# Perceiver block on one core: another order of the last product's parts on TensorE

## The chip, the cores and the metric

The kernel runs on one core of one Trainium2 chip. The metric is the device time of one execution in microseconds (us), as a median over runs. The core has five engines with queues of their own: TensorE (PE in the profile, its weight loads PEld), VectorE (DVE), ScalarE (ACT), GpSimd (POOL) and SyncE (SP, which issues the DMAs here). They meet by semaphores alone.

## The reference

Three residual steps over `x` of 2 batches x 128 rows x 2048 columns, all in float32: a product with a context after both were quantised, one layer of attention, and a product with 4-bit weights.

```python
x = x + xattn(layernorm(x), ctx)     # fake_quant(layernorm(x)) @ fake_quant(ctx)
x = x + attn(layernorm(x), Wq, Wkv, Wo)
# the last one, which the change is in:
zq = unpack4(qzeros, 2048) + 1
W = scales[g_idx] * (wq - zq[g_idx])           # 16 groups of 128 rows
x = x + (einsum('bsi,io->bso', layernorm(x), W) + bias)
```

## The kernel before, in words

TensorE multiplies in a rounded float32 format (FP32R). For accuracy each float32 operand is split in an upper part (the rounded value) and a lower part (the remainder), and a product is three matmuls: upper x upper, upper activations x lower weights, lower activations x upper weights. They add up in one PSUM bank (128 rows x 512 float32 columns; there are 8).

The last product has K = 2048 in 16 steps j of 128. Step j needs a **granule** of weights, 128 x 2048 upper (`hi_slots`) and 128 x 2048 lower (`lo_slots`), in a ring of five slots (four in `w_hi` and `w_lo`, the fifth in `xt_hi` and `xt_lo`). VectorE makes both: `ffn_upper(j)` (L865) multiplies the nibbles by the rounded scales, `ffn_lower(j)` (L870) by what the rounding left; they count `f_hi_set` and `f_lo_set`. ScalarE takes 8 off the nibbles before (L556). `hd_hi` and `hd_lo` hold the normalised rows, transposed: per batch 16 transposes on TensorE (`transposes`, L993) into four banks, ScalarE rounds each bank (L430), VectorE takes the remainder (L616).

One **granule of work**, `f_granule(j, b)`, is 12 matmuls of 128 x 512 for batch b: three parts of four matmuls, one for each 512-column chunk n, in bank 4b + n. The parts come in the order upper x upper, upper activations x lower weights, lower activations x upper weights. The last four matmuls of step 15 count `ffn_done`, one for each chunk. VectorE waits for each count, adds the bank to `resid` (L942), and SyncE stores the chunk (L336), 256 KB.

The zero points come in as a correction of low rank: `row_sums` (L1120, 32 matmuls of 128 x 256) sums the transposed rows by group into bank 7. Its first matmul waits until VectorE has written all of `hd_lo` for both batches. ScalarE reads the sums (L575), VectorE reads and combines them (L930, L931, which counts `rs_out`), and `correction` (L1144) multiplies them by a small table. Bank 7 also belongs to batch 1's last chunk, so `f_granule(0, 1)` waits for `rs_out`.

The order on each engine is written out by hand, as the order of the calls. On TensorE it is here: step 0 and step 1 of batch 0, the transposes of batch 1, the row sums, step 2 of batch 0, then (after `rs_out`) step 0 of batch 1, the correction, steps 1 and 2 of batch 1, steps 3 to 11 for both batches in turn, steps 12 to 15 of batch 0, steps 12 to 15 of batch 1. On VectorE `ffn_upper(2)` stands ahead of the four remainders of batch 1, `ffn_lower(2)` behind them.

Of the kernel before, what the change touches and what calls it, by code (L numbers as in the profile page):

```python
# [15 lines left out]
P = 128  # L16
B = 2
D = 2048
KT = D // P
CH = 512  # L20
NCH = D // CH
# [22 lines left out]
W_Q, W_O, W_F, W_END = 0, 16, 32, 48  # L44
# [4 lines left out]
def slot_of(w):  # L49

    return w % RING if w < W_O else (w - W_O) % (RING + 1)
# [14 lines left out]
def perceiver(nc, x, ctx_in, s1, z1, s2, z2, wq, wkv, wo, qweight, qzeros, scales, bias, out):  # L66
# [6 lines left out]
    with ExitStack() as ec:  # L73
        def sb(name, shape, dt):
            return ec.enter_context(nc.sbuf_tensor(name, shape, dt))

        def sem(name):
            return ec.enter_context(nc.semaphore(name))
# [22 lines left out]
        hd_hi = sb("hd_hi", [P, KT, B * P], F32R)  # L101
        with nc.sbuf_tensor("at", [P, KT, B * P], BF16) as at, nc.sbuf_tensor("q16", [P, 2, D], BF16) as q16:
            pass
        hd_lo = sb("hd_lo", [P, KT, B * P], F32R)
# [59 lines left out]
        hi_slots = [w_hi[:, s] for s in range(RING)] + [xt_hi[:].rearrange("p k m -> p (k m)")[:, 0:D]]  # L164
        lo_slots = [w_lo[:, s] for s in range(RING)] + [xt_lo[:].rearrange("p k m -> p (k m)")[:, 0:D]]
        raw_slots = [raw[:, s] for s in range(RING)] + [raw_fifth[:]]

        bank = ec.enter_context(nc.psum_tensor("bank", [P, 8, CH], F32))
# [44 lines left out]
        f_lo_set = sem("f_lo_set")  # L213
# [34 lines left out]
        ffn_done = sem("ffn_done")  # L248
# [11 lines left out]
        def tr_bank(n, g):  # L260
            if n == 0:
                return g % 3
            return 1 + g % 3 if n == 1 else 4 * (n % B) + g
# [682 lines left out]
        def _(pe):  # L946
            mm = nc.tensor.matmul
# [30 lines left out]
            def transposes(n):  # L978
                b = n % B
                pe.wait_ge(norm_set, n + 1)  # L980
                for t in range(KT):
                    g = t // 4
                    if n < B:
                        rows = work[:, b, :].rearrange("m (p t) -> m t p", t=KT)[:, t, :]
                    else:
                        h, r = divmod(t, PACK)
                        j = r // 2 + 4 * (r % 2)
                        rows = work[:, b, :].rearrange("m (h p j) -> m h j p", h=HALVES, j=PACK)[:, h, j, :]
                    if n < B and t == 12:
                        pe.wait_ge(lo_out, 4 * n + 1)  # L990
                    if n == 1 and t == 0:
                        pe.wait_ge(colsum_out, B)
                    ins = nc.tensor.transpose(bank[:, tr_bank(n, g), (t % 4) * P:(t % 4 + 1) * P], rows, ident[:])  # L993
                    if t % 4 == 3:
                        ins.then_inc(tr_done, 1)
# [119 lines left out]
            def row_sums():  # L1115
                pe.wait_ge(masks_set, 3)
                pe.wait_ge(lo_out, 4 * B + UNITS + 8)
                for k in range(KT):
                    for part in (hd_hi, hd_lo):
                        ins = mm(bank[:, 7, 0:B * P], group_of[:, k // PACK, :], part[:, k, :],  # L1120
                                 start=k == 0 and part is hd_hi, stop=k == KT - 1 and part is hd_lo)
                ins.then_inc(rs_done, 1)

            def f_granule(j, b):
                w, m = W_F + j, slice(b * P, (b + 1) * P)
                hi, lo = hi_slots[slot_of(w)], lo_slots[slot_of(w)]
                pe.wait_ge(f_hi_set, j + 1)
                pe.wait_ge(lo_out, 4 * B + UNITS + 4 * (b + 1))
                for left, right, first, last in ((hd_hi, hi, True, False), (hd_hi, lo, False, False),
                                                 (hd_lo, hi, False, True)):  # L1130
                    if right is lo:
                        pe.wait_ge(f_lo_set, j + 1)
                    for n in range(NCH):
                        ins = mm(bank[:, 4 * b + n, :], left[:, j, m], right[:, n * CH:(n + 1) * CH],  # L1134
                                 start=first and j == 0, stop=last and j == KT - 1)
                        if last and j == KT - 1:
                            ins.then_inc(ffn_done, 1)
                if b == B - 1 and j < KT - 1:
                    ins.then_inc(w_used, 1)

            def correction():
                for b in range(B):
                    for n in range(NCH):
                        mm(bank[:, 4 * b + n, :], rsum[:, b * P:(b + 1) * P], corr_r[:, n * CH:(n + 1) * CH],  # L1144
                           start=False, stop=False)
# [34 lines left out]
            for n in range(1, NCH):  # L1180
                ua, ub = 2 * n - 2, 2 * n - 1
                w = W_Q + 4 * n
# [49 lines left out]
            o_granule(15, 1)  # L1232

            f_granule(0, 0)
            f_granule(1, 0)
            transposes(3)
            row_sums()
            f_granule(2, 0)
            pe.wait_ge(rs_out, 1)
            f_granule(0, 1)  # L1240
            pe.wait_ge(corr_split, 1)
# [4 lines left out]
                f_granule(j, 0)  # L1246
                f_granule(j, 1)
            for b in range(B):
                for j in range(KT - 4, KT):
                    f_granule(j, b)  # L1250


_INS = ['x', 'ctx_4096', 'L0_xattn_x1_scale', 'L0_xattn_x1_zp', 'L0_xattn_x2_scale', 'L0_xattn_x2_zp',
# [19 lines left out]
```

## Time and profile before

| | before |
|---|---|
| median of 3 runs | 447.43 us |
| lowest, highest | 444.41, 447.49 us |
| profiled execution, its own time | 447.83 us |
| its span (first to last instruction) | 446.1 us |
| PE busy | 381.2 us (85%) |
| DVE busy | 322.4 us (72%) |
| ACT busy | 219.5 us (49%) |
| mean granted TensorE clock | 0.972 |

The span is shorter than the time by 1.7 us, which lie outside the first and last instruction. Busy shares are averages over stages with different limits. The last product fills the stretch from 344 us to the end.

### The profile page before, as it was taken

How to read it: one execution, taken by the hardware profiler on the slowest of the kernel's cores; microseconds unless marked ns; L12 is line 12 of the kernel's file. 1: busy time of each engine (PE TensorE's matmuls, PEld its weight loads, DVE VectorE, ACT ScalarE, POOL GpSimd, SP SyncE). 2: the span in 40 equal slices, each digit the busy share in tenths (PEclk: the TensorE clock that was granted, in tenths of full speed). 3: DMA queues.
4: the chain of work that ended last, by engine and by line, in shares of the span. 5: the costliest groups of instructions: out<-in, count | busy, mean ns of one | idle time of the engine just before them, and what ended most of it. 6: DMA issues, size and time to landing. Idle time of an engine off the chain costs nothing.

```text
span 446.1 us, 4684 instructions
## 1 busy us (share of the span) xinstructions
PE 381.2 (85%) x1836; PEld 280.8 (63%) x1836; DVE 322.4 (72%) x316; ACT 219.5 (49%) x266; POOL 38.2 (9%) x75
## 2 busy tenths in 40 slices
PE   0285667666999999999999999977989899999995
PEld 0121222213778886877877868855768788888884
DVE  4698896759702794794764948549999999999822
ACT  2887986993204595375573824123904233444000
POOL 8994000000000000000000001000000000000000
PEclk9999999969799999999999999988999999999999
DMA  6999999991035443443436416999400000000022
GB/s 284 423 422 421 405 412 424 422 389 70 1 97 205 181 153 131 131 154 122 162 133 244 135 54 157 195 250 389 180 1 1 1 0 0 1 0 1 0 94 94
DMA packets 24273, 77.43 MB, mean 174 GB/s; under 512 B 1626, under 2 KB 1802, under 8 KB 19210
## 3 DMA queue, kind: packets, MB, share of 16 engines
q1 hardware_dynamic: 24092, 77.01, 47.9%
q8 instruction: 14, 0.23, 0.2%
q10 hardware_dynamic: 160, 0.13, 0.1%
q14 instruction: 7, 0.06, 0.0%
HBM read 74.91 MB, written 2.10 MB: 173 GB/s over the span
## 4 chain that ended last, share of the span: by engine, by line
PE 57%; DMA 17%; DVE 9%; ACT 8%; SPq 5%; issue 4%; POOLq 0%; DVEq 0%; POOL 0%
PE bank L1134 19%; DMA raw<-in_ctx 11%; PE bank L1000 9%; PE bank L1002 9%; PE bank L1001 9%; DMA raw<-in_L_attn_Wo 5%; ACT q L417 4%; DVE w_lo L625 2%; PE bank L1062 2%; PE bank L1087 2%; SPq L325 2%; SPq L321 2%; PE bank L1075 1%; PE bank L1030 1%; DVE stats L595 1%
## 5 line engine op out<-in xcount | busy, mean ns | idle before, releaser
L625 DVE TENSOR_TENSOR w_lo<-raw,w_hi 128x2048 fp32r<-128x2048 f32 x29 | 66.2, 2283 | 23.1 <-ACT w_hi L437 23.1
L437 ACT ACTIVATE w_hi<-raw 128x2048 fp32r<-128x2048 f32 x29 | 55.3, 1911 | 38.2 <-DMA raw<-in_L_attn_Wo 22.7
L417 ACT ACTIVATE q<-raw,prm,inv 128x2048 uint8<-128x2048 f32 x32 | 66.1, 2090 | 11.8 <-DMA raw<-in_ctx 11.8
L1000 PE MATMUL bank<-w_hi,xt_hi 128*128 128x512 f32 x128 | 53.2, 416 | 4.6 <-DVE w_lo L625 4.6
L961 PE MATMUL bank<-q,at 128*128 128x512 bf16 x128 | 37.9, 424 | 21.3 <-DVE q L677 21.0
L1002 PE MATMUL bank<-w_hi,xt_lo 128*128 128x512 f32 x128 | 51.0, 398 | 0.0
L1001 PE MATMUL bank<-w_lo,xt_hi 128*128 128x512 f32 x128 | 50.9, 398 | 0.0
L1000 PE MATMUL bank<-w_hi,hd_hi 128*128 128x512 f32 x104 | 41.7, 401 | 4.1 <-DVE w_lo L625 4.1
L677 DVE TENSOR_SCALAR q<-q 128x2048 bf16<-128x2048 uint8 x32 | 38.5, 1225 | 7.5 <-ACT q L417 6.0
L1002 PE MATMUL bank<-w_hi,hd_lo 128*128 128x512 f32 x104 | 41.2, 397 | 0.0
L1001 PE MATMUL bank<-w_lo,hd_hi 128*128 128x512 f32 x104 | 41.2, 396 | 0.0
L461 ACT ACTIVATE work<-work,neg_mx 128x128 f32<-128x128 f32 x64 | 24.8, 389 | 23.4 <-DVE neg_mx L792 23.4
L961 PEld LDWEIGHTS bank<-q,at 128*128 128x128 bf16 x128 | 10.7, 103 | 40.2 <-DVE q L677 25.6
L1000 PEld LDWEIGHTS bank<-w_hi,xt_hi 128*128 128x128 f32 x128 | 24.6, 192 | 12.5 <-DVE w_lo L625 5.5
L556 ACT ACTIVATE work<-work 128x4096 bf16<-128x4096 uint16 x5 | 18.1, 3618 | 21.9 <-DVE work L858 21.9
L1002 PEld LDWEIGHTS bank<-w_hi,xt_lo 128*128 128x128 f32 x128 | 24.6, 192 | 5.5
L1134 PE MATMUL bank<-w_hi,hd_hi 128*128 128x512 f32 x104 | 27.8, 389 | 0.0
L1134 PE MATMUL bank<-w_hi,hd_lo 128*128 128x512 f32 x104 | 27.8, 389 | 0.0
L1134 PE MATMUL bank<-w_lo,hd_hi 128*128 128x512 f32 x104 | 27.8, 389 | 0.0
L1001 PEld LDWEIGHTS bank<-w_lo,xt_hi 128*128 128x128 f32 x128 | 24.7, 193 | 4.6 <-issue 0.2
L1000 PEld LDWEIGHTS bank<-w_hi,hd_hi 128*128 128x128 f32 x104 | 20.0, 192 | 9.8 <-DVE w_lo L625 5.0
L1002 PEld LDWEIGHTS bank<-w_hi,hd_lo 128*128 128x128 f32 x104 | 19.9, 192 | 4.3
(152 smaller groups left out, 654.2 us busy)
## 6 DMA issues: line engine op xcount, KB each, us to landing
raw<-in_ctx SPq DMA_DIRECT2D x32, 1024.0 KB, 8.3
raw<-in_L_attn_Wq SPq DMA_DIRECT2D x16, 1024.0 KB, 5.1
raw<-in_L_attn_Wo SPq DMA_DIRECT2D x13, 1024.0 KB, 6.1
raw_fifth<-in_L_attn_Wo SPq DMA_DIRECT2D x3, 1024.0 KB, 12.4
resid<-in_x SPq DMA_DIRECT2D x2, 1024.0 KB, 9.8
scale<-in_L_ffn_scales SPq DMA_DIRECT2D x16, 128.0 KB, 11.3
packed<-in_L_ffn_qweight SPq DMA_DIRECT2D x2, 1024.0 KB, 22.4
out_x<-resid SPq DMA_DIRECT2D x8, 256.0 KB, 2.9
```

The lines of the kernel that those rows point to most:

```text
L321: sp.dma_start(scale[i * PER_GROUP:(i + 1) * PER_GROUP, h, :], scales[g:g + 1, :].to_broadcast([PER_GROUP, D])).then_inc(scales_loaded, 16)
L417: nc.scalar.activation(q8[:, i % Q8], raw[:, i % RING, :], ACT.Identity, bias=prm[:, 3:4], scale=inv[:, 2:3]).then_inc(ctx_q, 1)
L437: nc.scalar.activation(hi_slots[s], raw_slots[s], ACT.Copy).then_inc(w_hi_set, 1)
L461: ins = nc.scalar.activation(prob[:, c], prob[:, c], ACT.Exp, scale=-1.0, bias=neg_mx[:, u % 2, h:h + 1], accum_out=den[:, u % 2, h:h + 1])
L556: nc.scalar.activation(values.bitcast(BF16), values.bitcast(U16), ACT.Copy, bias=-8.0).then_inc(d8_set, 1)
L625: nc.vector.tensor_tensor(lo_slots[s], raw_slots[s], hi_slots[s].bitcast(F32), ALU.subtract).then_inc(w_lo_set, 1)
L677: nc.vector.tensor_scalar(q16[:, i % 2], q8[:, i % Q8], -QSHIFT, None, ALU.add).then_inc(ctx_c, 1)
L961: mm(bank[:, 4 * b + n, :], at[:, k, b * P:(b + 1) * P], q16[:, i % 2, n * CH:(n + 1) * CH], start=start, stop=False)
L1000: mm(bank[:, out_bank, :], x_hi, hi[:, c], start=first, stop=False)
L1001: mm(bank[:, out_bank, :], x_hi, lo[:, c], start=False, stop=False)
L1002: return mm(bank[:, out_bank, :], x_lo, hi[:, c], start=False, stop=last)
L1134: ins = mm(bank[:, 4 * b + n, :], left[:, j, m], right[:, n * CH:(n + 1) * CH], start=first and j == 0, stop=last and j == KT - 1)
```

## The change

Nothing is computed otherwise; some of TensorE's instructions stand elsewhere in its queue. The other engines' queues are the same, instruction for instruction.

1. In every granule of work the lower weights come third instead of second, and with them the wait for `f_lo_set`.
2. In step 2 of batch 0 the row sums stand between the two parts on the upper weights and the part on the lower weights.
3. The last granule of each batch goes chunk by chunk: all three parts of chunk 0, its `ffn_done`, then chunk 1, and so on.

```diff
+            def f_part(j, b, n, part):
+
+                left, right = ((hd_hi, hi_slots), (hd_lo, hi_slots), (hd_hi, lo_slots))[part]
+                return mm(bank[:, 4 * b + n, :], left[:, j, b * P:(b + 1) * P],
+                          right[slot_of(W_F + j)][:, n * CH:(n + 1) * CH],
+                          start=part == 0 and j == 0, stop=part == 2 and j == KT - 1)
+
+            def f_by_upper(j, b):
                 pe.wait_ge(f_hi_set, j + 1)
                 pe.wait_ge(lo_out, 4 * B + UNITS + 4 * (b + 1))
-                for left, right, first, last in ((hd_hi, hi, True, False), (hd_hi, lo, False, False),
-                                                 (hd_lo, hi, False, True)):
-                    if right is lo:
-                        pe.wait_ge(f_lo_set, j + 1)
+                for part in range(2):
                     for n in range(NCH):
-                        ins = mm(bank[:, 4 * b + n, :], left[:, j, m], right[:, n * CH:(n + 1) * CH],
-                                 start=first and j == 0, stop=last and j == KT - 1)
-                        if last and j == KT - 1:
-                            ins.then_inc(ffn_done, 1)
-                if b == B - 1 and j < KT - 1:
+                        f_part(j, b, n, part)
+
+            def f_by_lower(j, b):
+                pe.wait_ge(f_lo_set, j + 1)
+                for n in range(NCH):
+                    ins = f_part(j, b, n, 2)
+                if b == B - 1:
                     ins.then_inc(w_used, 1)
+
+            def f_granule(j, b):
+                f_by_upper(j, b)
+                f_by_lower(j, b)
+
+            def f_last_granule(b):
+
+                pe.wait_ge(f_lo_set, KT)
+                for n in range(NCH):
+                    for part in range(3):
+                        ins = f_part(KT - 1, b, n, part)
+                    ins.then_inc(ffn_done, 1)
...
             transposes(3)
+            f_by_upper(2, 0)
             row_sums()
-            f_granule(2, 0)
+            f_by_lower(2, 0)
             pe.wait_ge(rs_out, 1)
             f_granule(0, 1)
...
             for b in range(B):
-                for j in range(KT - 4, KT):
+                for j in range(KT - 4, KT - 1):
                     f_granule(j, b)
+                f_last_granule(b)
```

TensorE's queue around the row sums, before: L993 are the transposes of batch 1, L1120 the row sums, L1134 first step 2 of batch 0 and then, from the row with `rs_out`, step 0 of batch 1.

```order
L993 MATMUL bank<-ident,work 128x128 [waits norm_set]
L993 MATMUL bank<-ident,work 128x128 x15
L1120 MATMUL bank<-hd_hi,group_of 128x256 [waits lo_out,masks_set]
L1120 MATMUL bank<-hd_lo,group_of 128x256
...
L1134 MATMUL bank<-w_hi,hd_hi 128x512 [waits lo_out,f_hi_set]
L1134 MATMUL bank<-w_hi,hd_hi 128x512 x3
L1134 MATMUL bank<-w_lo,hd_hi 128x512 [waits f_lo_set]
L1134 MATMUL bank<-w_lo,hd_hi 128x512 x3
L1134 MATMUL bank<-w_hi,hd_lo 128x512 x4
L1134 MATMUL bank<-w_hi,hd_hi 128x512 [waits lo_out,f_hi_set,rs_out]
```

The same place of the changed kernel (its L1127 is the matmul of `f_part`):

```order
L993 MATMUL bank<-ident,work 128x128 [waits norm_set]
L993 MATMUL bank<-ident,work 128x128 x15
L1127 MATMUL bank<-w_hi,hd_hi 128x512 [waits lo_out,f_hi_set]
L1127 MATMUL bank<-w_hi,hd_hi 128x512 x3
L1127 MATMUL bank<-w_hi,hd_lo 128x512 x4
L1120 MATMUL bank<-hd_hi,group_of 128x256 [waits lo_out,masks_set]
L1120 MATMUL bank<-hd_lo,group_of 128x256
...
L1127 MATMUL bank<-w_lo,hd_hi 128x512 [waits f_lo_set]
L1127 MATMUL bank<-w_lo,hd_hi 128x512 x3
L1127 MATMUL bank<-w_hi,hd_hi 128x512 [waits lo_out,f_hi_set,rs_out]
```

Eight matmuls moved from behind the row sums to ahead of them; between the row sums and the instruction that waits for `rs_out` four are left of twelve.

TensorE's last rows in the changed kernel, as they stand for chunks 0 and 1 of the last granule of batch 1 (before, its last row was four matmuls of `w_hi,hd_lo`, each of which counted `ffn_done`):

```order
L1127 MATMUL bank<-w_hi,hd_hi 128x512 [waits f_lo_set]
L1127 MATMUL bank<-w_hi,hd_lo 128x512
L1127 MATMUL bank<-w_lo,hd_hi 128x512
L1127 MATMUL bank<-w_hi,hd_hi 128x512
L1127 MATMUL bank<-w_hi,hd_lo 128x512
L1127 MATMUL bank<-w_lo,hd_hi 128x512
```

Each third matmul now ends a chunk and counts `ffn_done`.

## Rows read from the trace of the kernel before

**Rows 1.** Waits of PE, 322 to 447 us: who for whom, us in total, times, longest.
```profile
PE bank L1120 <- DVE hd_lo L616: 2.0, 1, 2.0
```

**Rows 2.** Chain that ended last, 318 to 447 us: start us, us, what.
```profile
364.67 75.49 PE bank L1134 x333
```

**Rows 3.** Timeline of PE around the row sums: start us, us, engine line op, [idle before].
```profile
349.42 1.95 PE L993 MATMUL bank<-ident,work 128*128 128x128 f32 x16
353.32 0.36 PE L1120 MATMUL bank<-hd_hi,group_of 128*128 128x256 f32 x1 [1.95 <-DVE hd_lo L616]
...
357.11 0.28 PE L1120 MATMUL bank<-hd_lo,group_of 128*128 128x256 f32 x1
357.23 1.09 PE L1134 MATMUL bank<-w_hi,hd_hi 128*128 128x512 f32 x4
...
359.98 1.07 PE L1134 MATMUL bank<-w_hi,hd_hi 128*128 128x512 f32 x4
```

**Rows 4.** Timeline of DVE, same stretch.
```profile
348.36 2.29 DVE L865 TENSOR_TENSOR w_hi<-work,scale_hi 128x2048 fp32r<-128x2048 bf16 x1
350.69 2.48 DVE L616 TENSOR_TENSOR hd_lo<-bank,hd_hi 128x512 fp32r<-128x512 f32 x4
...
357.94 0.48 DVE L930 TENSOR_SCALAR kv_t<-bank,one_row 128x256 f32<-128x256 f32 x1 [1.43 <-ACT k_t L575]
358.46 0.48 DVE L931 SCALAR_TENSOR_TENSOR rsum<-k_t,part_lo,kv_t 128x256 fp32r<-128x256 f32 x1
358.86 2.28 DVE L865 TENSOR_TENSOR xt_hi<-work,scale_hi 128x2048 fp32r<-128x2048 bf16 x1
```

**Rows 5.** Timeline of ACT, same stretch.
```profile
357.43 0.48 ACT L575 ACTIVATE k_t<-bank,one_row 128x256 fp32r<-128x256 f32 x1 [5.30 <-PE bank L1120]
```

**Rows 6.** Timeline of PE behind the transposes of batch 0.
```profile
336.58 2.07 PE L993 MATMUL bank<-ident,work 128*128 128x128 f32 x16
338.41 0.48 PE L1000 MATMUL bank<-xt_hi,hd_hi 128*128 128x512 f32 x1
338.73 0.39 PE L1001 MATMUL bank<-xt_lo,hd_hi 128*128 128x512 f32 x1
338.96 0.40 PE L1002 MATMUL bank<-xt_hi,hd_lo 128*128 128x512 f32 x1
```

**Rows 7.** Timeline of PE in the steady part: step 3 and the last granule.
```profile
369.95 1.07 PE L1134 MATMUL bank<-xt_hi,hd_hi 128*128 128x512 f32 x4
...
437.95 1.07 PE L1134 MATMUL bank<-w_hi,hd_hi 128*128 128x512 f32 x4
...
439.76 1.07 PE L1134 MATMUL bank<-w_hi,hd_lo 128*128 128x512 f32 x4
```

**Rows 8.** Timeline of DVE at the end.
```profile
419.60 2.28 DVE L870 TENSOR_TENSOR w_lo<-work,scale 128x2048 fp32r<-128x2048 bf16 x1
...
440.19 2.48 DVE L942 TENSOR_TENSOR resid<-bank,resid 128x512 f32<-128x512 f32 x4 [8.40 <-PE bank L1134]
```

**Rows 9.** Timeline of SP's queue: first and last store of batch 1.
```profile
440.91 0.33 SPq L336 DMA_DIRECT2D out_x<-resid  x1
...
442.70 0.33 SPq L336 DMA_DIRECT2D out_x<-resid  x1
```

**Rows 10.** Source view of L336, the eight stores of 256 KB.
```profile
DMA to landing us min/median/max: 2.5/2.9/3.0
```

**Rows 11.** Timeline of PE, a first matmul after an idle stretch.
```profile
304.21 0.50 PE L1000 MATMUL bank<-w_hi,hd_hi 128*128 128x512 f32 x1 [2.70 <-DVE w_lo L625]
```

**Rows 12.** Windows: us, PE, PEld, DVE, ACT, POOL busy (instructions), PEclk, DMA share, GB/s.
```profile
305.30:308.50 3.20, 3.20 (x9) 2.52 (x8) 3.17 (x2) 1.70 (x1) 0.00 (x0) 0.50 0.99 374
308.80:312.00 3.20, 3.20 (x16) 2.60 (x15) 3.17 (x3) 1.34 (x1) 0.00 (x0) 1.00 1.05 385
353.30:363.00 9.70, 9.68 (x58) 8.70 (x59) 8.23 (x6) 3.98 (x2) 0.00 (x0) 1.00 0.01 2
```

More of the change, by code:

```diff
@@ L1122, in row_sums @@
                 ins.then_inc(rs_done, 1)
-            def f_granule(j, b):
-                w, m = W_F + j, slice(b * P, (b + 1) * P)
-                hi, lo = hi_slots[slot_of(w)], lo_slots[slot_of(w)]
+            def f_part(j, b, n, part):
[4 more added lines that the diff above has]
+            def f_by_upper(j, b):
                 pe.wait_ge(f_hi_set, j + 1)
                 pe.wait_ge(lo_out, 4 * B + UNITS + 4 * (b + 1))
-                for left, right, first, last in ((hd_hi, hi, True, False), (hd_hi, lo, False, False),
-                                                 (hd_lo, hi, False, True)):
-                    if right is lo:
-                        pe.wait_ge(f_lo_set, j + 1)
+                for part in range(2):
                     for n in range(NCH):
-                        ins = mm(bank[:, 4 * b + n, :], left[:, j, m], right[:, n * CH:(n + 1) * CH],
-                                 start=first and j == 0, stop=last and j == KT - 1)
-                        if last and j == KT - 1:
-                            ins.then_inc(ffn_done, 1)
-                if b == B - 1 and j < KT - 1:
-                    ins.then_inc(w_used, 1)
+                        f_part(j, b, n, part)
[4 more added lines that the diff above has]
+                if b == B - 1:
+                    ins.then_inc(w_used, 1)
+            def f_granule(j, b):
[7 more added lines that the diff above has]
+                    ins.then_inc(ffn_done, 1)
             def correction():
```

## The prediction

> **What bounds the kernel now.** The change touches the last product alone, so I read that stretch, 344 us to the end. The chain of waits comes first [rows 2]: one piece of 75.49 us is 333 matmuls of L1134 in a row, so from 364.67 us to the end of the products TensorE is never waiting. The list of TensorE's waits [rows 1] then holds a single one in the stretch that the edit touches: the row sums wait 2.0 us for VectorE's last remainder (its other two belong to the product before). The timelines of the engines say where that wait lies and what stands around it [rows 3 to 5]; those of the end show what follows the last matmul [rows 7 to 9]. Only TensorE's queue changes, so a gain has to come from one of three places: a wait for lower weights, the idle stretch before the row sums, or the tail behind the last matmuls.
>
> The pace first. Step 3 of batch 0 starts at 369.95 and the last granule at 437.95 [rows 7]. Between them lie 9 steps for both batches, steps 12 to 15 of batch 0 and 12 to 14 of batch 1: 25 granules of 12, 300 matmuls, in 68.00 us, so **0.2267 us a matmul**. The durations in the rows (0.39 for one, 1.07 for four) overlap and aren't added.
>
> **Lower weights third (edit 1).** It postpones the need for lower weights by four matmuls, 0.91 us, in every granule. It pays only where they are late. Upper weights of step 3 are begun on VectorE at 358.86 and take some 2.2 us, the lower ones as long behind them, so both are there by 363.3 [rows 4]; TensorE wants them at 369.95 [rows 7], 6.6 us later. The last lower ones are done at 419.60 + 2.28 = 421.9 [rows 8], and step 15 of batch 0 stands four granules before 437.95, at 427.1. No wait is there to remove: 0. It can't lose either: same instructions, the same number of weight loads, and the slot is freed at the granule's end as before.
>
> **Row sums between the parts (edit 2).** Before: the transposes of batch 1 start at 349.42, the row sums at 353.32 after 1.95 us idle [rows 3]. The transposes hold the queue for 338.41 - 336.58 = 1.83 us, and a 128x512 matmul behind them takes 338.73 - 338.41 = 0.32 to the next instead of 0.23 [rows 6]. Now the eight matmuls on the upper weights of step 2 start at 349.42 + 1.83 = 351.25. Their weights are finished at 348.36 + 2.29 = 350.65 [rows 4]: 0.6 us early. They end their turn at 351.25 + 0.32 + 7 x 0.2267 = 353.16. The last remainder ends at 350.69 + 2.48 = 353.17, and the row sums start, as before, at about 353.32. So **eight matmuls (1.81 us) fit in the idle stretch, nearly exactly**; they write banks 0 to 3 while VectorE reads 4 to 7.
>
> From there the row sums run unchanged to 357.23 [rows 3]. Behind them only the four matmuls with lower weights are left, 0.93 us with the change of shape, to 358.16. The next granule needs `rs_out`. ScalarE reads the sums at 357.43 [rows 5], VectorE takes 357.94 to 358.42 and 358.46 to 358.94 [rows 4], and its message needs about 0.1 us (353.17 to 353.32 is the same step, 0.15). So TensorE gets on at 359.05 instead of 359.98, less 0.09 for a first matmul behind a wait, as above (0.32 for 0.23). **Gain 0.84 us.** The other 0.9 us of the 1.81 turn into a new wait, in front of batch 1's first granule: it was covered by eight matmuls that now lie elsewhere. Queued behind it are only TensorE's own products; VectorE waits for none of them, as its next weights go into slots that are free for long. Bounds: 0.5, if a message takes 0.3 us more; 1.81, if the new wait weren't there. The rows of the two VectorE steps are this kernel's own, so I take 0.84.
>
> **Last granule by chunks (edit 3).** Before: the last four matmuls start at 439.76, the first add at 440.19, that is 0.43 behind the matmul that ends its chunk [rows 7, 8]. The four adds stand back to back, to 440.19 + 2.48 = 442.67, so VectorE is the end of the chain, not TensorE: its last matmul ends at 439.76 + 1.07 = 440.83. Now chunk n ends with matmul 3n + 3 of twelve. The last starts at 437.95 + 11 x 0.2267 = 440.44, so its add at 440.87. The three others start 0.68 us apart from 438.83 on, and an add takes 0.60 in a row, 0.68 alone (2.48 = 3 x 0.60 + 0.68): each is over as the next is due. The last ends at 441.55 instead of 442.67: **1.12 us**. The last store goes out at once as now (442.70 after 442.67) [rows 9]. Batch 0's last granule does the same 10.9 us earlier, off the path.
>
> Is the end set by the last store or by the sum of the four? The last is issued at 442.70 and the span ends at 446.1; its time to landing lies within 2.5 to 3.0 us [rows 9, 10]. If the four together set it, the first counts: it would go out at 438.83 + 0.68 + 0.03 = 439.54 instead of 440.91, 1.37 us earlier. The bounds are 1.12 and 1.37. I take 1.12, because the last of four lands no later after its issue than the others do. The Trainium skill, page "DMA: Bandwidth & Descriptors", section "Anatomy of one DMA", says that a DMA costs about 2.0 us fixed, plus its bytes at 436 GB/s, which is 2.6 us for 256 KB as an estimate; by it each store ends so long after its own issue, and the gain would be 1.12. The landing times of 2.5 to 3.0 us bear that out roughly, the upper ones not quite.
>
> Writing one bank three times in a row isn't slower: the product before does so with all twelve of its matmuls, and its spacing is 338.96 - 338.73 = 0.23 [rows 6], as with changing banks.
>
> **Sum.** 0 + 0.84 + 1.12 = 1.96 us. The profiled execution had 447.83, the median is 447.43, 0.4 lower. From 447.43 this gives **445.5 us**, 0.4% less. A difference under 1% is about what a measurement of this kernel can't tell from none: its three runs alone lie 3 us apart.
>
> **Rivals.**
>
> *Both upper bounds (5%).* 1.81 + 1.37 = 3.2, 444.2 us. For it: the idle stretch is long enough. Against: the two VectorE steps between row sums and `rs_out` are in the rows.
>
> *The message path eats edit 2 (9%).* `rs_out` is 0.8 us later, because ScalarE or VectorE is held up by the matmuls that now run beside other work, or the eight matmuls push the row sums back (their cover is 0.01 us, so every delay ahead of them counts). Only the tail is left: 446.3.
>
> *The change doesn't do what it says (2%).* If edit 2's matmuls had to wait for step 2's upper weights, the row sums behind them in the queue would wait as well. VectorE makes these weights directly before the remainders that the row sums need, so it would take a second wait. 447.
>
> *Slower: TensorE's clock (4%).* An idle stretch can be followed by the lower clock. After one of 2.70 us the granted clock read 0.50, 1.2 GHz, from about 305.3 to 308.5 [rows 11, 12]: 9 matmuls ran there where 16 ran in the same 3.2 us at full clock, so one such stretch costs 7 x 0.2267 = 1.6 us when nothing hides it. The idle stretch before the row sums, 1.95 us, was followed by full clock [rows 12]. Now it is gone, and one of 0.9 us stands 5 us later. It decides only if that shorter one, with the 0.15 us before the row sums, triggers a drop that the longer didn't, and twice: 445.5 + 3.2 = 448.7; once would be 447.1. The Trainium skill, page "TensorE: Matmul & The Clock Gate", section "The HAM clock gate", says that the default state is the throttled one and that only activity releases it; by this rule less idle time makes a drop less likely, so the trace's direction and the page's agree against this rival.
>
> *Another level (12%).* One of the three runs shows 444.41, 3 us under the others, about two stretches at the lower clock. The stages before 344 us have several and aren't touched. If the runs of the changed kernel have that luck more often, their median is 442.5 to 444.
>
> The forecast itself has 68%, with a range of its own of 444.5 to 446.3. With the cases around it the range is **442.9 to 447.1**: it takes in the rivals on both sides except the lower end of the last and a clock drop taken twice. Faster by over 1% means under 442.96: half of the last rival, 7%. Slower by over 1% means over 451.9, more than three stretches at the lower clock: 1%. Within 1%: 92%.
>
> **What would show it.** Edit 1: no wait for lower weights in either trace, and the same 0.2267 us from step 3 on. Edit 2: TensorE's idle time before the row sums falls from 1.95 to about 0.15 us, the row sums still start at 353.3, and a new wait for VectorE's L931 of 0.8 to 0.9 us stands before step 0 of batch 1, all later products 0.84 us earlier. Edit 3: four adds 0.68 us apart with small idle gaps, the last ending 0.7 us behind TensorE's last matmul instead of 1.84, the last store 1.96 us earlier in all, and the end 3.4 us behind it. Wrong I would be if the row sums start later than 353.5, if the last add starts more than 0.3 us behind the end of the last matmul, or if a stretch at the lower clock shows up behind 344 us.

## The result and the profile after

The changed kernel takes 445.52 us in the median of 12 runs (444.53 to 447.52), the kernel before 448.23 us in 12 runs, three of which are those of the table before. One of these twelve took 762.16 us, and the ratio is formed without it. The ratio of the two is **0.9952, 95% interval 0.9932 to 0.9972**: 0.5% faster, by 2.1 us, with 1.96 us forecast; the medians alone lie 2.7 us apart. A second set of runs gave 0.9945, interval 0.9926 to 0.9964.

The profiled execution has a span of 445.6 us, only 0.5 less than before. Most of what was gained is hidden in it by something else: batch 1's transposes start at 351.13 instead of 349.42, 1.71 us later. Ahead of them only steps 0 and 1 of batch 0 are changed (the order of edit 1), and from the first of their matmuls to the transposes it is 351.13 - 345.68 = 5.45 us, as before (349.42 - 343.97). So the shift is older than the last product. The windows view of the stretch from 40 to 130 us (us, busy us and instructions of PE, PEld, DVE, ACT, POOL, granted clock, DMA share, GB/s), first of the kernel before:

```profile
40.00:130.00 90.00, 63.94 (x309) 31.16 (x309) 64.79 (x75) 59.17 (x38) 0.96 (x1) 0.91 0.71 285
```

and of the changed one:

```profile
40.00:130.00 90.00, 69.56 (x310) 31.88 (x310) 65.50 (x78) 58.90 (x38) 0.96 (x1) 0.83 0.71 284
```

The instructions are the same (one or two fall on the border), the granted clock is lower, 0.83 for 0.91. SP's first row behind that stretch says that 1.50 us of the 1.71 are there already; before:

```profile
134.84 67.00 SPq L299 DMA_DIRECT2D raw<-in_L_attn_Wq  x10
```

and changed:

```profile
136.34 67.00 SPq L299 DMA_DIRECT2D raw<-in_L_attn_Wq  x10
```

The clock and the delay go together here, but the clock doesn't settle where the last product begins: the run with edit 1 alone (below) has 0.83 and 136.44 too, and its transposes start at 349.94. In the second profile of the same changed kernel the clock of the stretch is 0.91 again, the transposes start at 349.23 and the span is 443.8 us. So spans of two executions can't be compared more closely than to 2 us, and everything below is measured as **distances inside a trace**: from batch 1's transposes to step 3, and from step 3 to the end.

TensorE's waits from 318 us on, changed kernel (who for whom, us in total, times, longest):

```profile
PE bank L1000 <- DVE xt_lo L625: 1.5, 1, 1.5
PE bank L1000 <- DVE w_lo L625: 1.4, 1, 1.4
PE bank L1127 <- DVE rsum L931: 0.7, 1, 0.7
```

The wait of the row sums [rows 1] is gone, a wait for `rs_out` (L931) has come. The timeline of PE around them, which answers to [rows 3]:

```profile
351.13 1.95 PE L993 MATMUL bank<-ident,work 128*128 128x128 f32 x16
352.84 1.18 PE L1127 MATMUL bank<-w_hi,hd_hi 128*128 128x512 f32 x4
353.85 1.08 PE L1127 MATMUL bank<-w_hi,hd_lo 128*128 128x512 f32 x4
355.04 0.36 PE L1120 MATMUL bank<-hd_hi,group_of 128*128 128x256 f32 x1
...
358.94 1.09 PE L1127 MATMUL bank<-w_lo,hd_hi 128*128 128x512 f32 x4
360.72 1.20 PE L1127 MATMUL bank<-w_hi,hd_hi 128*128 128x512 f32 x4 [0.68 <-DVE rsum L931]
361.75 1.08 PE L1127 MATMUL bank<-w_hi,hd_lo 128*128 128x512 f32 x4
...
370.84 1.07 PE L1127 MATMUL bank<-xt_hi,hd_hi 128*128 128x512 f32 x4
```

The row sums start 3.91 us behind the transposes, before 353.32 - 349.42 = 3.90: they didn't move, and eight matmuls now lie in what was idle time. Behind them stand four matmuls and then the new wait. Step 3 starts 370.84 - 351.13 = 19.71 us behind the transposes, against 369.95 - 349.42 = 20.53 [rows 3, 7]: **0.82 us**.

The end of the timelines of DVE, PE and SP, one fence for each (they answer to [rows 7 to 9]; the first row of SP's is all four stores of batch 1 together, the second the last of them):

```profile
439.72 2.73 DVE L942 TENSOR_TENSOR resid<-bank,resid 128x512 f32<-128x512 f32 x4 [8.15 <-PE bank L1127]
```

```profile
438.84 0.39 PE L1127 MATMUL bank<-w_hi,hd_hi 128*128 128x512 f32 x1
...
441.34 0.39 PE L1127 MATMUL bank<-w_lo,hd_hi 128*128 128x512 f32 x1
```

```profile
440.44 2.37 SPq L336 DMA_DIRECT2D out_x<-resid  x4
...
442.48 0.33 SPq L336 DMA_DIRECT2D out_x<-resid  x1
```

The four adds take 2.73 us from start to end instead of 2.48, since each waits a little for its chunk, but they begin 0.88 us after the last granule does (438.84) instead of 2.24. The last ends at 442.45, 0.72 us behind TensorE's last matmul (441.34 + 0.39), where it was 1.84. From step 3 to the end of the span it is 445.6 - 370.84 = 74.76 us, before 446.1 - 369.95 = 76.15: **1.39 us**, known to 0.1 at worst, since spans are given to 0.1. (The trace itself has the two spans as 445.628 and 446.096, which gives 1.36.) Of this, 1.11 lie up to the last store's issue (442.48 - 370.84 = 71.64, before 442.70 - 369.95 = 72.75). The rest is behind it: 445.6 - 442.48 = 3.12 us instead of 3.40 [rows 9].

| distance, us | before | changed |
|---|---|---|
| transposes to row sums | 3.90 | 3.91 |
| transposes to step 3 | 20.53 | 19.71 |
| last matmul's end to last add's end | 1.84 | 0.72 |
| last store's issue to end of span | 3.40 | 3.12 |
| step 3 to end of span | 76.15 | 74.76 |

### The profile page after: what moved, and what is told of

Its sections match the earlier page's. It is cut to its first block, busy times and chain, and to the rows that moved or that the text cites. A ratio compares the mean times of both kernels' runs of the same rounds, so it can differ in the third digit from the quotient of the medians.

```text
span 445.6 us, 4682 instructions
## 1 busy us (share of the span) xinstructions
PE 388.6 (87%) x1836; PEld 282.2 (63%) x1836; DVE 323.0 (72%) x316; ACT 219.5 (49%) x266; POOL 37.0 (8%) x75
## 4 chain that ended last, share of the span: by engine, by line
PE 62%; DMA 12%; DVE 10%; ACT 7%; SPq 5%; issue 3%; POOLq 0%; POOL 0%; DVEq 0%; ACTq 0%
PE bank L1127 19%; PE bank L1000 9%; PE bank L1001 9%; PE bank L1002 9%; DMA raw<-in_ctx 6%; DMA raw<-in_L_attn_Wo 5%; PE bank L961 4%; ACT q L417 3%; PE bank L1062 2%; DVE w_lo L625 2%; SPq L325 2%; PE bank L1087 2%; SPq L321 2%; PE bank L1075 1%; DVE q L677 1%
## 5 line engine op out<-in xcount | busy, mean ns | idle before, releaser
L961 PE MATMUL bank<-q,at 128*128 128x512 bf16 x128 | 43.0, 471 | 18.5 <-DVE q L677 18.3
L1000 PE MATMUL bank<-w_hi,hd_hi 128*128 128x512 f32 x104 | 42.0, 404 | 4.5 <-DVE w_lo L625 4.5
L1001 PE MATMUL bank<-w_lo,hd_hi 128*128 128x512 f32 x104 | 41.1, 395 | 0.0
L961 PEld LDWEIGHTS bank<-q,at 128*128 128x128 bf16 x128 | 11.7, 111 | 39.8 <-DVE q L677 21.4
L1127 PE MATMUL bank<-w_hi,hd_hi 128*128 128x512 f32 x104 | 29.0, 392 | 0.7 <-DVE rsum L931 0.7
L1127 PE MATMUL bank<-w_lo,hd_hi 128*128 128x512 f32 x104 | 28.8, 390 | 0.0
L1127 PE MATMUL bank<-w_hi,hd_lo 128*128 128x512 f32 x104 | 28.8, 390 | 0.0
L1000 PEld LDWEIGHTS bank<-w_hi,hd_hi 128*128 128x128 f32 x104 | 19.9, 192 | 10.0 <-DVE w_lo L625 5.3
L1127 PEld LDWEIGHTS bank<-w_hi,hd_hi 128*128 128x128 f32 x104 | 19.4, 188 | 5.0 <-DVE rsum L931 1.1
```

The source lines that it names most:

```text
L961: mm(bank[:, 4 * b + n, :], at[:, k, b * P:(b + 1) * P], q16[:, i % 2, n * CH:(n + 1) * CH], start=start, stop=False)
L1000: mm(bank[:, out_bank, :], x_hi, hi[:, c], start=first, stop=False)
L1001: mm(bank[:, out_bank, :], x_hi, lo[:, c], start=False, stop=False)
L1127: return mm(bank[:, 4 * b + n, :], left[:, j, b * P:(b + 1) * P], right[slot_of(W_F + j)][:, n * CH:(n + 1) * CH], start=part == 0 and j = ...
```

## The experiments

Two questions: do the three edits contribute as the steps of the prediction said (0, 0.84, 1.12), and what cuts the moved matmuls' 1.81 us to 0.82 and adds 0.28 to the tail's gain? The first four runs were measured on one chip beside 29 runs of the kernel before (448.18 us), the other four on another chip beside 23 (448.09 us); each ratio is to the runs on its own chip.

### Edit 1 alone

```diff
-for left, right, first, last in ((hd_hi, hi, True, False), (hd_hi, lo, False, False),
-                                 (hd_lo, hi, False, True)):
+for left, right, first, last in ((hd_hi, hi, True, False), (hd_lo, hi, False, False),
+                                 (hd_hi, lo, False, True)):
```

> Edit 1 alone: the lower weights third in every granule of the last product, nothing else. My theory: no wait for lower weights was there, so the time is that of the kernel before (within 0.2 us in the trace), the row sums still start 9.35 us behind the last but one granule's start as before, after 1.95 us idle, and step 3 follows at the same distance. Rival (the gain of 0.5% came from looser waits on VectorE): 1 to 2 us faster.

Measured: ratio 0.9971 to the kernel before, interval 0.9947 to 0.9994. In the trace the distance from the transposes to step 3 is 370.47 - 349.94 = 20.53 us and step 3 to the end 446.6 - 370.47 = 76.1, both as before. Its waits, same view as above:

```profile
PE bank L1120 <- DVE hd_lo L616: 2.0, 1, 2.0
PE bank L1000 <- DVE w_lo L625: 1.4, 1, 1.4
PE bank L1000 <- DVE xt_lo L625: 1.3, 1, 1.3
```

They are those of the kernel before. The edit changes nothing that the last product shows. (The expectation's 9.35 us is the distance from the start of step 0 of batch 0 to the row sums, and it names the granule wrongly; the view from the transposes says the same.) The ratio's interval just leaves out 1, and from it alone one would have credited the edit with 0.3%. But no distance in the last product is shorter for it, and nothing ahead of the last product was edited. The rival's way, looser waits on VectorE, is out; the 0.3% I take for the spread between executions seen above, without having shown it. The three runs with one edit each came out at 0.9971, 0.9967 and 0.9967, though their traces differ by 0.0, 0.8 and 1.4 us from the kernel before: the ratios don't tell the edits apart, and what follows on their shares rests on the traces.

### Edit 2 alone

```diff
...
+            f_split(2, 0, lambda hi, lo: ((hd_hi, hi), (hd_lo, hi)))
             row_sums()
-            f_granule(2, 0)
+            f_split(2, 0, lambda hi, lo: ((hd_hi, lo),))
             pe.wait_ge(rs_out, 1)
```

> Edit 2 alone: the two parts of step 2, batch 0, on the upper weights ahead of the row sums, the part on the lower ones behind; the order in all other granules and the tail as before. My theory: step 3 starts 0.84 to 0.9 us earlier relative to the transposes of batch 1, with a new wait of 0.7 us for L931 (the changed kernel shows 0.68); time 0.8 to 0.9 us under before. Rival (the moved matmuls are worth their full length): 1.8 us. Rival (the new wait eats it): 0.

Measured: ratio 0.9967, interval 0.9941 to 0.9993. The cut lines define `f_split`, which does the named parts of one granule. The timeline of PE (L1150 is its matmul):

```profile
350.53 1.95 PE L993 MATMUL bank<-ident,work 128*128 128x128 f32 x16
...
358.34 1.09 PE L1150 MATMUL bank<-w_lo,hd_hi 128*128 128x512 f32 x4
360.12 1.21 PE L1134 MATMUL bank<-w_hi,hd_hi 128*128 128x512 f32 x4 [0.68 <-DVE rsum L931]
...
370.26 1.07 PE L1134 MATMUL bank<-xt_hi,hd_hi 128*128 128x512 f32 x4
```

370.26 - 350.53 = 19.73 us to step 3, 0.80 less than before, with the same new wait of 0.68. From step 3 to the end it is 76.2, as before. So edit 2 brings its 0.8 us without the other two. Both rivals, 1.8 and 0, fall.

### Edit 3 alone

```diff
+            def f_last_granule(b):
...
+                for n in range(NCH):
+                    for left, right, last in ((hd_hi, hi, False), (hd_hi, lo, False), (hd_lo, hi, True)):
+                        ins = mm(bank[:, 4 * b + n, :], left[:, KT - 1, m], right[:, n * CH:(n + 1) * CH],
+                                 start=False, stop=last)
+                    ins.then_inc(ffn_done, 1)
...
-                for j in range(KT - 4, KT):
+                for j in range(KT - 4, KT - 1):
                     f_granule(j, b)
+                f_last_granule(b)
```

> Edit 3 alone: the last granule of each batch chunk by chunk. My theory: the last add ends 0.7 us behind the end of TensorE's last matmul instead of 1.84, and the stores land a little sooner after their issue (3.1 instead of 3.4 us from the last issue to the end, as in the changed kernel): 1.1 to 1.4 us under before. Rival (the four stores are limited together by their bytes): the end follows the first store, 1.4 us, and the distance from last issue to the end grows instead of falling.

Measured: ratio 0.9967, interval 0.9946 to 0.9989. Transposes to step 3: 370.92 - 350.40 = 20.52, as before. Step 3 to the end: 445.7 - 370.92 = 74.78, so 1.37 us less. DVE and SP at the end:

```profile
439.80 2.73 DVE L942 TENSOR_TENSOR resid<-bank,resid 128x512 f32<-128x512 f32 x4 [8.15 <-PE bank L1147]
```

```profile
442.56 0.33 SPq L336 DMA_DIRECT2D out_x<-resid  x1
```

The last issue is at 442.56 and the end 3.14 us behind it. This is within what both sides expected in size (1.1 to 1.4), and the distance behind the last issue fell, which the rival had said would grow. That part of the rival was thought out wrongly: with stores issued 0.68 us apart instead of 0.60, the last has less of its neighbours in front of it, not more. What limits the stores is the question of two runs below. Edits 2 and 3 alone sum to 0.80 + 1.37 = 2.17 us, both together gave 0.82 + 1.39 = 2.21: to within the 0.1 of the spans they don't interact.

### Nine matmuls ahead of the wait for rs_out

```diff
             f_by_lower(2, 0)
-            pe.wait_ge(rs_out, 1)
-            f_granule(0, 1)
+            for n in range(NCH):
+                if n == NCH - 1:
+                    pe.wait_ge(rs_out, 1)
+                for part in range(3):
+                    ins = f_part(0, 1, n, part)
+            ins.then_inc(w_used, 1)
```

> The changed kernel, but in step 0 of batch 1 the nine matmuls of chunks 0 to 2 (banks 4 to 6) stand ahead of the wait for rs_out, and only chunk 3 (bank 7) behind it. My theory: the new wait of 0.68 us was the whole price of edit 2's cut gain; nine matmuls (2.04 us) cover it, no wait for L931 is left, and step 3 starts 0.8 to 0.9 us earlier than in the changed kernel relative to the transposes: time about 0.8 us under the changed kernel, 2.9 under before. Rival (the matmuls in banks 4 to 6 hold up ScalarE's and VectorE's reads of bank 7): L575, L930 and L931 take longer than 0.48 us each, and the gain is smaller.

Measured: 444.37 us (443.93 to 446.6, 6 runs), ratio 0.9916 to the kernel before, interval 0.9884 to 0.9948. The timeline of PE:

```profile
349.04 1.95 PE L993 MATMUL bank<-ident,work 128*128 128x128 f32 x16
350.75 1.17 PE L1127 MATMUL bank<-w_hi,hd_hi 128*128 128x512 f32 x4
351.76 1.08 PE L1127 MATMUL bank<-w_hi,hd_lo 128*128 128x512 f32 x4
352.95 0.35 PE L1120 MATMUL bank<-hd_hi,group_of 128*128 128x256 f32 x1
...
356.85 1.09 PE L1127 MATMUL bank<-w_lo,hd_hi 128*128 128x512 f32 x4
357.78 0.39 PE L1127 MATMUL bank<-w_hi,hd_hi 128*128 128x512 f32 x1
...
367.76 1.07 PE L1127 MATMUL bank<-xt_hi,hd_hi 128*128 128x512 f32 x4
```

and ScalarE's and VectorE's readings of bank 7:

```profile
357.05 0.47 ACT L575 ACTIVATE k_t<-bank,one_row 128x256 fp32r<-128x256 f32 x1 [5.30 <-PE bank L1120]
```

```profile
357.56 0.48 DVE L930 TENSOR_SCALAR kv_t<-bank,one_row 128x256 f32<-128x256 f32 x1 [1.42 <-ACT k_t L575]
358.08 0.48 DVE L931 SCALAR_TENSOR_TENSOR rsum<-k_t,part_lo,kv_t 128x256 fp32r<-128x256 f32 x1
```

Step 3 is 18.72 us behind the transposes: 1.81 less than before, 8 x 0.2267, the whole length of the eight matmuls, and 0.99 less than in the changed kernel (0.8 to 0.9 expected). That is more than the wait's 0.68. The record counts a wait from the end of the matmul in front, 358.94 + 1.09 = 360.03. Without one, the next granule would have started at 358.94 + 0.93 = 359.87 (0.93 is 357.78 - 356.85 in this run) and not at 360.72: 0.85 us. Its first four matmuls then took 361.75 - 360.72 = 1.03 to the next ones instead of 0.91 [rows 7], 0.12 more for a start from idle. Together that is 0.97 of the 0.99. The three readers of bank 7 take 0.47 and 0.48 us as before, with matmuls in banks 0 to 6 beside them. So the new wait was all that kept edit 2 from its upper bound.

### All of step 2 ahead of the row sums

```diff
-            f_by_upper(2, 0)
+            f_granule(2, 0)
             row_sums()
-            f_by_lower(2, 0)
```

> The changed kernel, but all of step 2 of batch 0 ahead of the row sums, the part on the lower weights too. Its weights are made by VectorE behind the remainders, so TensorE's queue stands at them. My theory: the row sums start 7.0 us behind the start of batch 1's transposes instead of 3.9, because the lower weights of step 2 are there at 6.0; the wait for rs_out grows to 1.8 us; step 3 starts 22.85 us behind the transposes, against 19.71 in the changed kernel and 20.53 before. Time 3.1 us over the changed kernel and about 1 us over the kernel before. Rival (the lower weights third and the split don't matter, as long as work fills the idle stretch): as the changed kernel.

Measured: 449.09 us, ratio 1.0032 to the kernel before, interval 1.0012 to 1.0053: slower, by 1.4 us, 1 expected. The timeline of PE:

```profile
349.13 1.95 PE L993 MATMUL bank<-ident,work 128*128 128x128 f32 x16
...
355.14 1.20 PE L1127 MATMUL bank<-w_lo,hd_hi 128*128 128x512 f32 x4 [2.21 <-DVE w_lo L870]
356.18 0.27 PE L1120 MATMUL bank<-hd_hi,group_of 128*128 128x256 f32 x1
...
361.76 1.20 PE L1127 MATMUL bank<-w_hi,hd_hi 128*128 128x512 f32 x4 [1.60 <-DVE rsum L931]
...
371.88 1.07 PE L1127 MATMUL bank<-xt_hi,hd_hi 128*128 128x512 f32 x4
```

The row sums start 7.05 us behind the transposes (7.0 expected), the two waits are 2.21 and 1.60 (1.8 expected for the second), and step 3 comes 22.75 us behind them (22.85 expected), 3.04 more than in the changed kernel. Here the cut between upper and lower parts is worth 3 us: the lower weights of step 2 are made behind the remainders that the row sums need, so whatever needs them must stand behind the row sums.

### The kernel before with one store at the end

```diff
-                    sp.dma_start(out[b, :, c], resid[:, b, c]).then_inc(stored, 16)
+                    if b == 0 or n == NCH - 1:
+                        sp.dma_start(out[b, :, c], resid[:, b, c]).then_inc(stored, 16)
-            sp.wait_ge(stored, 16 * B * NCH)
+            sp.wait_ge(stored, 16 * (NCH + 1))
```

This kernel leaves chunks 0 to 2 of batch 1 unwritten; it serves to measure the last store alone.

> The kernel before, with the stores of chunks 0 to 2 of batch 1 left out (their output stays unwritten), so that batch 1's last store moves alone. It separates what the tail is limited by. If the last store's own latency sets the end (my prediction's value): 3.40 us from its issue to the end of the span, as before. If the four stores set it together by their bytes (the prediction's upper bound, which the changed kernel's tail of 1.39 us speaks for): clearly less, 2.8 to 3.1 us.

Measured: ratio 0.9983, interval 0.9966 to 0.9999. The last row of SP's queue, in a span of 444.6 us:

```profile
441.69 0.33 SPq L337 DMA_DIRECT2D out_x<-resid  x1
```

444.6 - 441.69 = 2.9 us from issue to end, where four stores in a row leave 3.40. So 0.5 us of the tail before comes from the three stores in front of the last. The adds are as before (2.48 us for the four), and the stores are all that was edited. Where the stores hold each other up, in SP's queue, in the DMA engines or at the memory, isn't shown.

### Steps 12 to 15 of batch 1 by chunk

This is edited on top of the kernel with nine matmuls ahead of the wait.

```diff
-            for b in range(B):
-                for j in range(KT - 4, KT - 1):
-                    f_granule(j, b)
-                f_last_granule(b)
+            for j in range(KT - 4, KT - 1):
+                f_granule(j, 0)
+            f_last_granule(0)
+            for n in range(NCH):
+                for j in range(KT - 4, KT):
+                    for part in range(3):
+                        ins = f_part(j, 1, n, part)
+                ins.then_inc(ffn_done, 1)
```

> The kernel with free banks first, and steps 12 to 15 of batch 1 all chunk by chunk: 12 matmuls a chunk, so chunks end 2.72 us apart instead of 0.68. Same matmuls and adds. The three earlier stores are then through before the last goes out. Theory (four stores share the tail by their bytes): from TensorE's last matmul to the end of the span 0.3 to 0.6 us less than with the last granule alone by chunk. Rival (the last store's own latency sets the end): no change.

Measured: 444.17 us (443.07 to 445.61, 6 runs), ratio 0.9918, interval 0.9897 to 0.9940. The end of DVE and of SP's queue, in a span of 442.4 us:

```profile
436.10 0.69 DVE L942 TENSOR_TENSOR resid<-bank,resid 128x512 f32<-128x512 f32 x1 [2.03 <-PE bank L1127]
438.81 0.69 DVE L942 TENSOR_TENSOR resid<-bank,resid 128x512 f32<-128x512 f32 x1 [2.03 <-PE bank L1127]
```

```profile
439.53 0.33 SPq L336 DMA_DIRECT2D out_x<-resid  x1
```

From the last issue to the end it is 2.9 us, as with a store that moves alone. Before it VectorE waits 2.03 us for each chunk, and the stores go out 2.7 us apart. That is 0.3 us less than the 3.2 in the trace of the kernel with nine matmuls ahead of the wait, whose last store goes out at 439.40 in a span of 442.6. From TensorE's last matmul the gain is 0.3 to 0.4 us, as expected: 442.4 - (438.39 + 0.39) = 3.6 here, 442.6 - (438.25 + 0.39) = 4.0 there. In time that is below what the runs tell apart (0.9918 against 0.9916). It is the lowest median of all, and both versions with nine matmuls ahead are faster than the kernel before. Their medians also lie 1 us under the changed kernel's 445.5, but the intervals overlap with its own; that the 0.99 us is there rests on the traces.

### The changed kernel again

> The changed kernel once more, as the yardstick on this chip: 0.5% under the kernel before; distance from batch 1's transposes to step 3 19.7 us, from step 3 to the end 74.8 us, as in its first trace.

Measured: 445.48 us, ratio 0.9945, interval 0.9926 to 0.9964; 19.73 us from the transposes to step 3 (19.71 in the first trace) and 74.8 from there to the end. The distance between instructions repeats to 0.02 us, the span (443.8 for 445.6) does not.

## Why the prediction was right, step by step

- **Edit 1, forecast 0:** 0.00 in both distances of the run with it alone. Step 3's lower weights were ready 6.6 us ahead in the rows, and the same in the run (made by 361.58 + 2.29 = 363.87, wanted at 370.47).
- **Edit 2, forecast 0.84:** 0.82 in the changed kernel, 0.80 alone. Each piece came as worked out: row sums unmoved at 3.91 us behind the transposes, `rs_out` deciding the next granule. The wait was forecast at 0.8 to 0.9 us and is recorded as 0.68; the gap between starts is 360.72 - 359.87 = 0.85, and the record counts only from the end of the last matmul in front of it. The cover of 0.01 us between the eight matmuls and the last remainder held: both ran at the pace that the rows had given, and the row sums didn't move.
- **Edit 3, forecast 1.12:** 1.39. Up to the last store's issue 1.11 was right to 0.01. The step that failed is the one that read "the last of four lands no later after its issue than the others do" and took the lower bound. The last did land sooner after the edit, because stores close together hold each other up: alone, a store leaves 2.9 us to the end, with three 0.60 us apart in front of it 3.4, and with three 0.68 us apart 3.12. The trace before had it: the source view of L336 with a window round one store gives that store's landing time alone, counted from behind its 0.33 us of issue. Batch 1's first store before the change:

```profile
DMA to landing us min/median/max: 2.5/2.5/2.5
```

  its last:

```profile
DMA to landing us min/median/max: 3.0/3.0/3.0
```

  and the last in the changed kernel:

```profile
DMA to landing us min/median/max: 2.7/2.7/2.7
```

  So the last of four did land later after its issue than the first, by 0.5 us, and the range of 2.5 to 3.0 in [rows 10] was this order and not scatter. The term of the sum that was too small is the 1.12. The upper bound, the first store's issue, was the better one here: it went out 440.44 - 370.84 = 69.60 us behind step 3 instead of 440.91 - 369.95 = 70.96, which is 1.36 us, and 1.39 was measured. The Trainium skill's fit from "DMA: Bandwidth & Descriptors", section "Anatomy of one DMA", about 2.0 us fixed plus bytes at 436 GB/s, is given there for DMAs that GpSimd issues; these go out from SyncE. Its 2.6 us as an estimate for 256 KB lies near the 2.5 us in which a store alone lands. It says nothing of the 0.5 us that neighbours add; with several stores in flight the measurement speaks against using it for each by itself.
- **The other rivals.** No stretch at the lower clock appeared in the last product, as the windows view of the changed kernel from 344 to 440 us has it (its columns are those of [rows 12]); the clock is the 1.00.

```profile
344.00:440.00 96.00, 95.22 (x443) 79.19 (x442) 80.69 (x54) 28.05 (x13) 0.00 (x0) 1.00 0.04 11
```

  The other level of 444.41 us wasn't one of the changed kernel's own: its runs lie between 444.53 and 447.52. What moves whole executions by 2 us lies ahead of 344 us, where the granted clock differs between profiles of the same code; that the clock is the whole cause isn't shown. (The prediction gives "faster by over 1%" half of this rival's 12%; that is 6%, not its 7%.)

That the median fell 0.02 us from the forecast of 445.5 is luck in part. The forecast started from 447.43, the median of three runs, and twelve runs gave 448.23; from there it would have been 446.3. What bears the prediction out is the difference: 1.96 us forecast, 2.21 by the traces, 2.1 by the ratio.

The change itself is explained: 0.82 + 1.39 = 2.21 us by the traces (2.18 with the finer spans), 0.5% by the runs. What stays open is why the runs with edit 1 alone came out 0.3% under the kernel before, with nothing in the trace of the last product for it.

## What to carry to other kernels

Moving work into an idle stretch pays in full only if the work isn't the cover of the next wait: here eight of twelve matmuls covered a message path of 1.8 us through two engines, and half of their length came back as a new wait, until work on banks that the path doesn't touch took their place. Where an engine in order waits for a producer in order, cut the work so that what stands ahead of a wait needs only what the producer makes first. At the end, finish outputs one after the other at the pace at which they are added and stored: stores close together hold up the last one, so it counts how early the first goes out and how far apart they are.

For gains under 1%, measure distances between instructions inside a trace: they repeated to 0.02 us where spans of the same kernel differed by 1.8.

## What the runs showed of the hardware

- A 256 KB store takes 2.9 us from its issue to the end of the span when it is alone, 3.4 us behind three others 0.60 us apart. By landing times it is 2.5 us for the first of such a row and 3.0 for the last.
- Reads of one PSUM bank by ScalarE and VectorE (0.47 and 0.48 us for 128x256) weren't slowed by matmuls that wrote other banks meanwhile.
- Three matmuls in a row into one bank run at the same 0.227 us as four into four banks: step 3 to TensorE's last matmul is 441.34 - 370.84 = 70.50 us with the last granule by chunk, which is 311 x 0.2267. Twelve in a row into one bank do too: 438.39 - 367.89 = 70.50 us with steps 12 to 15 of batch 1 by chunk.
